# Two cross attentions of a four-layer decoder: which engine copies each turned head, and when, and where the result's turn stands

## The reference

```python
def _L1_xattn_ref(memory, query, b, seq_len):        # 16 heads
    k_mem, v_mem = jnp.split(memory, 2, axis=2)
    Q = _split_heads(query, NUM_HEADS) * dh ** (-0.5)
    Kh = _split_heads(k_mem, NUM_HEADS)
    Vh = _split_heads(v_mem, NUM_HEADS)
    logits = jnp.einsum('bhqd,bhkd->bhqk', Q, Kh) + b
    valid = (jnp.arange(S)[None, :] < seq_len[:, 0:1]).astype(jnp.float32)
    logits = logits + MASK_VALUE * (1.0 - valid)[:, None, None, :]
    weights = jax.nn.softmax(logits, axis=-1)
    out = jnp.einsum('bhqk,bhkd->bhqd', weights, Vh)
    return out.transpose(0, 2, 1, 3).reshape(B, S, UNITS)
...
x = x + _L1_xattn_ref(ctx_2048, _layernorm(x, axis=-1), L1_xattn_b, itok_Bx1_68_817)
...
x = x + _L2_xattn_ref(ctx_2048, _layernorm(x, axis=-1), mask_BxS2_ik0, L2_xattn_b)   # the same with 8 heads
```

## Time and profile before

| | us |
|---|---|
| median of 3 runs | 2337.86 (2336.58 to 2340.95) |
| the profiled execution, its own time | 2337.4 |
| its span, first to last instruction | 2335.3 |
| PE busy | 1972.2 (84%) |
| DVE busy | 1494.3 (64%) |
| ACT busy | 1078.4 (46%) |
| POOL busy | 752.9 (32%) |
| phase 4, first scores to last values | 941 to 1172 |
| phase 7, first scores to last values | 1681 to 1808 |

### The profile page before, as it was taken

The page is one execution under the profiler, slowest core; times in us unless marked ns, Lnnn a source line. Parts: engine busy times, 40 slices in busy tenths (PEclk is TensorE's granted clock), DMA queues, the critical chain, the costliest instruction groups (busy, mean ns, idle before and its releaser), DMA issues.

```text
span 2335.3 us, 34887 instructions
## 1 busy us (share of the span) xinstructions
PE 1972.2 (84%) x11970; PEld 1349.9 (58%) x11970; DVE 1494.3 (64%) x4706; ACT 1078.4 (46%) x2641; POOL 752.9 (32%) x780
## 2 busy tenths in 40 slices
PE   4888888998999999787669999667788798988679
PEld 3554556776565554555435778556655456666546
DVE  7666536545565567787521777689777855777763
ACT  2333343555433332666511465668676323666332
POOL 3122134110222232225450365465443322021353
PEclk9999998999999999999779999888899989999899
DMA  6999702000100002101151355400230100000100
GB/s 242 333 337 326 236 1 86 19 19 1 59 1 1 1 1 88 47 19 50 45 215 51 109 145 156 161 0 1 75 121 12 37 1 17 2 1 2 39 0 37
DMA packets 40302, 180.63 MB, mean 77 GB/s; under 512 B 6816, under 2 KB 24352, under 8 KB 36992
## 3 DMA queue, kind: packets, MB, share of 16 engines
q1 hardware_dynamic: 32496, 157.30, 19.9%
q0 software_dynamic: 7632, 21.11, 2.6%
HBM read 155.19 MB, written 98.89 MB: 109 GB/s over the span
## 4 chain that ended last, share of the span: by engine, by line
PE 60%; DVE 20%; ACT 10%; issue 4%; POOL 3%; another core or an unknown queue 2%; DMA 0%; DVEq 0%; POOLq 0%; SPq 0%; ACTq 0%
PE ps L217 39%; PE ps L740 4%; ACT BIG L817 4%; PE ps L712 3%; PE ps L759 3%; PE ps L2008 2%; DVE BIG L780 2%; ACT BIG L292 2%; PE ps L282 2%; PE ps L2020 1%; DVE BIG L292 1%; DVE XN L273 1%; PE ps L846 1%; DVE SML L258 1%
## 5 line engine op out<-in xcount | busy, mean ns | idle before, releaser
L217 PE MATMUL ps<-BIG 128*128 128x256 f16 (+2 forms) x1616 | 337.4, 358 | 27.1 <-DVE BIG L2619 12.9
L817 ACT ACTIVATE BIG<-BIG,SML 128x256 f32<-128x256 f32 (+1 forms) x768 | 302.6, 482 | 21.0 <-DVE SML L780 20.8
L217 PEld LDWEIGHTS ps<-BIG 128*128 128x128 f16 (+1 forms) x1616 | 221.0, 138 | 121.4 <-issue 65.5
L292 ACT ACTIVATE BIG<-ps 128x512 f32<-128x512 f32 (+1 forms) x288 | 154.0, 569 | 239.3 <-PE ps L740 187.5
L740 PE MATMUL ps<-CST,BIG 128*128 128x128 f32 x1408 | 218.3, 291 | 54.5 <-ACT BIG L817 41.1
L740 PEld LDWEIGHTS ps<-CST,BIG 128*128 128x128 f32 x1408 | 162.7, 147 | 128.1 <-ACT BIG L817 88.5
L637 POOL TENSOR_TENSOR BIG<-BIG 128x512 f16<-128x512 f32 x120 | 142.3, 1187 | 276.9 <-ACT BIG L571 248.6
L217 PE MATMUL ps<-XN,BIG 128*128 128x512 f16 x864 | 203.0, 390 | 14.4 <-ACT BIG L548 5.5
L780 DVE CUSTOM_DVE_ANT_0 BIG<-ps,BIG 128x256 f32<-128x256 f32 x512 | 181.2, 420 | 33.1 <-PE ps L712 24.4
L221 POOL TENSOR_SCALAR SML<-SML 128x4 f32<-128x4 f32 (+1 forms) x96 | 25.8, 269 | 491.0 <-DVE SML L261 212.3
L217 PE MATMUL ps<-WA,XT 128*128 128x256 f32 (+2 forms) x576 | 143.2, 392 | 27.2 <-DVE X L2178 7.1
(11 more groups left out here) (413 smaller groups left out, 3834.7 us busy)
## 6 DMA issues: line engine op xcount, KB each, us to landing
slots<-in_zeros SPq DMA_DIRECT2D x28, 2640.0 KB, 64.2
WA<-slots SPq DMA_DIRECT2D x95, 132.0 KB
BIG<-in_l1e SPq DMA_DIRECT2D x2, 4224.0 KB
BIG<-spread SPq DMA_DIRECT2D x16, 512.0 KB, 6.0
BIG<-in_l0e SPq DMA_DIRECT2D x8, 768.0 KB, 8.1
BIG<-in_ctxT SPq DMA_DIRECT2D x8, 512.0 KB, 6.3
BIG<-in_ctxT SPq DMA_DIRECT2D x16, 256.0 KB, 3.1
BIG<-in_ctx SPq DMA_DIRECT2D x16, 256.0 KB, 3.4
```

What stands on the lines that cost most here:

```text
L217: m = T.e.matmul(ps, l, r, start=i == 0, stop=i == len(pairs) - 1)
L292: return q.e.activation(o, i, ACT.Copy) if q is A else q.e.tensor_copy(o, i)
L817: A.e.activation(s[:, q, 0:kn[q]], s[:, q, 0:kn[q]], ACT.Exp, bias=mx[:, q:q + 1], scale=-1.0).then_inc(*(A.sig("exp", p, n, i) if q else ...
```

## The change

`by` becomes a list of strings, one for each quad in turn, and differs in phases 4 and 7: ("VAAV", "VAAA", "VAAA", "VAAV") for the four quads of a batch in phase 4, ("VAAV", "VAAA") for the two in phase 7. ScalarE copies heads 1 and 2 always, and head 3 in the "VAAA" quads; VectorE copies head 0, and head 3 in the others. VectorE's copy of head 3 of quad n-1 moves from before the maxima of quad n to behind them. `values_pe` now waits for all four copies by name. `post_at` shifts the result's turn on PE from the third and fourth move after a batch's last values to the fifth and sixth, which puts it behind the values of the next step; the division on DVE shifts by two moves in phase 4 and by one in phase 7. In phase 7 later pauses are shortened by the same number, in phase 4 they are not, so that all that follows there comes two moves later. `second_late=(2,)` defers, in the third quad of each batch of phase 4, the turn of head 1 to the next step, behind the next scores.

```diff
-        def attend(p, nh, quads, kn, get, pt=None, by="VVAA", va=None):
+        def attend(p, nh, quads, kn, get, pt=None, by=("VVAA",), va=None, post_at=(2, 4, 0, 0), second_late=()):
...
                 if 1 <= n <= c["np"]:
+                    if (n - 1) % ppb in c["second_late"]:
+                        turn_pe(c, n - 1, 1)
                     turn_pe(c, n - 1, 2)
                     turn_pe(c, n - 1, 3)
...
                     turn_pe(c, n, 0)
                     side.move()
-                    turn_pe(c, n, 1)
+                    if j not in c["second_late"]:
+                        turn_pe(c, n, 1)
...
-            waits(T, ("pt", p, n, 1), ("pt", p, n, 3))
+            waits(T, *[("pt", p, n, i) for i in range(4)])
...
                 evac_pt(V, c, n - 1, 2)
-                evac_pt(V, c, n - 1, 3)
                 if n < c["np"]:
...
                                 *(V.sig("max", p, n, i) if q else V.step()))
+                evac_pt(V, c, n - 1, 3)
                 side.move()
                 evac_pt(V, c, n, 0)
...
-            if not 0 <= n < c["np"] or c["by"][i] != ("A" if q is A else "V"):
+            if not 0 <= n < c["np"] or c["by"][n % len(c["by"])][i] != ("A" if q is A else "V"):
...
-            yield from pause(2)
+            yield from pause(c["post_at"][0])
             waits(T, ("o", p, b, 0), ("o", p, b, 1))
...
-                c = attend(p, 16, quads, [2 * P, 2 * P], get, spare_ring(), va=below)
+                c = attend(p, 16, quads, [2 * P, 2 * P], get, spare_ring(), ("VAAV", "VAAA", "VAAA", "VAAV"), below, post_at=(4, 6, 0, 0), second_late=(2,))
...
-                c = attend(p, 8, [range(0, 4), range(4, 8)], [2 * P, 2 * P], get, va=below)
+                c = attend(p, 8, [range(0, 4), range(4, 8)], [2 * P, 2 * P], get, None, ("VAAV", "VAAA"), below, post_at=(4, 5, 2, 1), second_late=())
...
-                yield from pause(8 if pairs is not None else 11)
+                yield from pause(8 if pairs is not None else 11 - c["post_at"][2])
...
         def post_out_dve(c, b, projected):
             p = c["p"]
-            yield from pause(4)
+            yield from pause(c["post_at"][1])
...
-                yield from pause(2)
+                yield from pause(2 - c["post_at"][3])
```

More of the change, by code:

```diff
@@ L647, in pause @@
                 yield
-        def attend(p, nh, quads, kn, get, pt=None, by="VVAA", va=None):
+        def attend(p, nh, quads, kn, get, pt=None, by=("VVAA",), va=None, post_at=(2, 4, 0, 0), second_late=()):
             w = 512 // nh
-            c = dict(p=p, nh=nh, w=w, dh=256 // nh, quads=quads, kn=kn, ppb=len(quads), np=B * len(quads), by=by)
+            c = dict(p=p, nh=nh, w=w, dh=256 // nh, quads=quads, kn=kn, ppb=len(quads), np=B * len(quads), by=by,
+                     post_at=post_at, second_late=second_late)
             c["SM"] = [get(512).rearrange("p (q k) -> p q k", q=2) for _ in range(8)]
@@ L904, in shared_1 @@
             c = attend(1, 8, [range(0, 4), range(4, 8)], [2 * P, 2 * P], scratch((0, 3072), (5632, 6656)),
-                       lambda n: spare.pop() if spare else own(n), "AAAA", scratch((3328, 5376)))
+                       lambda n: spare.pop() if spare else own(n), ("AAAA",), scratch((3328, 5376)))
             get = scratch((11776, 12800), (13824, 14848))
```

## The result

| | before | after |
|---|---|---|
| median, in turn on one chip | 2337.22 us (2333.99 to 2340.95, 4 runs) | 2312.43 us (2308.03 to 2315.73, 4 runs) |
| span of the profiled execution | 2335.3 | 2313.6 |

The account below looks back on a forecast made before the run. A chain of waits through PE, ACT and DVE was taken to bound the attention quads, with no engine full. From 2337.4, phase 4 gives 18 and phase 7 gives 9: 2310.4, predicted 2310, range 2296 to 2330.

Parts of the forecast that it names:

- The chain through three engines: Phase 4 attention: no engine is full; PE, ACT and DVE wait in turn, 5.08 us a quad, 7.15 once a batch.
- the rival of the busiest engine: PE's matmuls, not waits for ACT, pace the quads; at most 11 us gained, 2332 to 2337; chance 0.08.
- The clean batch, 22.39 to 19.65.: Phase 4's second, third and fifth batches: quads of 4.60, 4.66, 5.24 and 5.15, saving 2.7 us a batch.
- The wait of 1.42 goes, because the result is copied right behind the exponentials.: Phase 4: PE's result turn no longer waits 1.42 us for ACT's copy, made behind the previous step's exponentials.
- The router batches, 2.5 and 3.5.: Phase 4's fourth and sixth batches, with router work on DVE, save 2.5 and 3.5 us.
- VectorE becomes the bound: Rival: DVE paces phase 7 and phase 4's fourth, sixth and last batches; only 15 us gained, 2322; chance 0.22.
- Phase 7, -9.: Phase 7: 12.75 to 11.1 us a pair of quads by the walk; 1.4 taken in each of six batches, 9 in all.
- What is saved reaches the end: Fences stand on both sides of phases 4 and 7 and no load is late, so their savings shorten the whole.
- The stalls: Idle beside phase 4's scatters, -20 to +20 us, none in the sum; rivals: grow, 2345, chance 0.06; shrink, 2300, chance 0.14.
- something that these DMAs hold up: Phase 4: something held up by POOL's scatters reaches ACT and DVE; ACT idles unnamed 29.9 us in seven pieces.
- The signs: Confirming: second-batch score groups 4.6 to 5.3 apart, no 1.42 wait, ACT's 42.2 idle halved, DVE over 90% in phase 7.
- those against it: Refuting: third quad still 7, turns waiting over 0.5 for `ob` or VectorE's copies, ACT's unnamed idle leaving 20 to 40 us.

Follow-up runs that it names:

- the second pair: Kernel before and changed kernel, both unaltered, profiled again on a second chip: spans 2288.9 and 2263.5 us; the changed kernel's ratio there 0.9898.
- the first pair: The original profiled executions of the kernel before and the changed kernel: spans 2335.3 and 2313.6 us.
- the last four experiments: Against the kernel before: changed kernel with router products two moves earlier, 0.9874; also without deferral, 0.9880; phase 4's scatters moved to phase 5, before 1.0068, changed 0.9948.

## Why the prediction was right, point by point

**What bounds it.** The chain through three engines was read rightly. PE's work stayed what it was, and the time fell by 1.1%, so the rival of the busiest engine (2332 to 2337) is out. In the clean batch PE's busy share rose from 84% to 92% with the same work, so it was waits that went. Over the program the turns wait less for exponentials, 36.9 for 41.1, but not less in all (54.4 for 54.5 in the earlier trace rows); other waits took the place:

```profile
L744 PE MATMUL ps<-CST,BIG 128*128 128x128 f32 x1408 | 217.0, 290 | 54.4 <-ACT BIG L821 36.9
```

**The clean batch, 22.39 to 19.65.** The walk for two copies on ACT held to 0.06 in the first and second quads. The batch came out at 20.24. The term at fault is the third and fourth quads of this batch, 10.39 forecast, 11.01 measured: the walk gave DVE maxima, a copy and two divisions, and left out the norm's 1.7 us of statistics, which the old third quad covered. Elsewhere the two take 10.4. The fifth batch is 20.5 for another reason, the router's last work in its first quad (5.48 for 4.60).

**"The wait of 1.42 goes, because the result is copied right behind the exponentials."** True of the whole change, and false without the deferred turn: alone, or with the copies, the turn's move puts a wait of 1.41 for the division's bank in its place. The copies (20 us alone) did more than the turn (9).

**The router batches, 2.5 and 3.5.** This step failed: 0.2 and 0.7. The prediction took half a clean batch's gain for "DVE becomes the late one". It took every matmul at the length of its row before, and gave the clock no term. In the fourth batch the same matmuls keep PE busy 27.2 us for 24.6, in the sixth, without a stall, 24.5 for 21.4, and the batches miss their forecasts by 2.3 and 3.0. With the whole clock and head 1 not deferred the fourth batch is 25.9. That is 3.7 under the kernel before, but the kernel before had rows at the lower clock itself:

```profile
1010.75 2.09 PE L712 MATMUL ps<-BIG 32*128 32x256 f32 x16
1012.77 1.76 PE L740 MATMUL ps<-CST,BIG 128*128 128x128 f32 x8
```

With these at their 1.15 and 1.09, before would be some 28.0, an estimate from rows, and the gain at equal clock about 2.1 of the 2.5 forecast. So most of what is missing stands beside the lower clock. Why it is lower in the new order is open, and a kernel that holds it up in these batches wasn't tried. The wait of 1.13 for the division's bank, which the prediction also left out, is in the slow and in the fast fourth batch, so it isn't what parts them. The rival "VectorE becomes the bound" (2322) wasn't met, in the clean batches or in phase 7; in a router batch DVE set the length only with the products moved earlier.

**Phase 7, -9.** -8.7 in the loop, but not as 1.4 a batch, as shown above. DVE isn't over 90% busy in the batches shown (85, 81 and 70%); PE is, with 95 and 94% in the first two. The walk's 12.75 and 11.1 us a batch are near the first batch before (12.4) and the second after (10.9), but the seven average 14.3 and 13.0. It didn't describe most batches, so that the difference came out right is partly luck. The loop's end gives some back: the norm's turn waits for POOL, and the last scores to the last result's turn go from 19.1 to 21.4.

```profile
1779.54 1.97 PE L282 MATMUL ps<-CST,XN 128*128 128x128 f32 x8 [3.53 <-POOL XN L273]
```

The prediction's allowance for this was 0.3, for statistics that wait for POOL's addition.

**"What is saved reaches the end"** held in the second pair: 14.3 and 8.6 in the two loops and 2.7 between them make 25.6, and 25.4 arrive. In the first pair 4.2 came between the phases and 3.4 were lost behind phase 7, for a reason that stays open. Inside phase 5, which no edit touches and where 32 scatters run, PE stands still with no releaser, 4.38 and 3.78 us ahead of two groups of products before, 2.99 and 2.42 after.

That the total of 27 came within 2.2 of the first measurement (24.8) is in part luck: phase 4 gave 5.4 less than its share, and a part of the rest came between the phases, where the sum had nothing.

**The stalls** neither grew nor shrank: 40.3 us for the three quads before, 40.8 after. The range's 10 us either way was wide enough, and the true spread lies between chips. The "something that these DMAs hold up" is there on the chips that are slower for every kernel; on the two others the same scatters stop nothing.

**The signs.** Of those that would show it, the distances of the second batch (4.60 to 5.84, forecast 4.6 to 5.3) and the gone wait of 1.42 came, in phase 7 too. ACT's idle before its copies didn't halve (42.2 to 41.8; a third less on the second chip, 45.7 to 29.7), and DVE isn't over 90% busy. Of those against it, two came true while the time came out right: turns wait up to 0.7 for a division (phase 7) and up to 2.3 for a copy of VectorE's (phase 4), over the 0.5 that it named, and the unnamed idle of ACT left 20 to 40 us (13.8). The second was a poor sign: the stalls were still there, with a part of them put down to other waits.

## What to carry to other kernels

When an order written by hand is shifted, list every instruction that shares a rotation of banks with the moved one and walk them all: here the division, the router's products and a turn use three banks, and a wait taken from one reappears on the next. Give each quad its own sum of VectorE's work, with every norm and router instruction in it. Switch off the parts of a change one at a time and read single batches, not only the total: here the turn's move is worth something in a clean batch only with the deferral. And compare batches at the same granted clock before a lost gain is put down to a wait: the same batch took 25.9 us at the whole clock and 29.5 at 0.84.

## What the runs showed of the hardware

The same kernel before takes 2337 us in its first runs, 2334 on the chip of the last four experiments, and 2295 and 2294 on two others (whether the first two are one chip isn't known). Of the 46.4 us between the two traces of it, 19.1 lie in phase 4 and 25.3 between phase 4 and 7, the stretches with indirect scatters; phase 7 is the same to 0.1. In the slower trace ACT and DVE stand still in phase 4 for up to 9.3 us at a time with no releaser, in phase 5 for up to 16.1, and PE for up to 4.9; in the faster one the same scatters run beside them and nothing stops. Where the stalls occur they come with the scatters: on the chip of the last four experiments phase 4 has none once its scatters are moved. But the scatters aren't enough: eight traces on the two faster chips have the same scatters in phase 4 and no stall. What in the chip or the execution makes the difference is open. The Trainium skill (Runtime: NRT & Kernel Launch, Instruction fetch mechanics) says that instructions are fetched by a DMA queue of each engine's own, mostly hidden; it doesn't speak of stalls beside scatters. The instruction packets between 1060 and 1180 us take 0.3 to 1.6 us each in the slower and in the faster trace alike, which speaks against slow packets and doesn't exclude late ones.

The clock moves whole batches. In phase 7 the changed kernel takes 98.8 to 99.0 in three traces and, with phase 7's code untouched, 97.2 to 97.4 in five others, all with another phase 4 ahead of it (PE busy 86.5 to 86.7 and 85.0 to 85.3, clock 0.95 and 0.96).
